# One attention and mixture-of-experts layer: POOL normalises the contexts from a copy that ScalarE makes, and VectorE takes only the reciprocal

## The reference

```
result = embeddings @ w_qkv                      # q, k, v
scores = einsum('bnqd,bnkd->bnqk', q, k) / sqrt(h)
probs  = softmax(scores, axis=-1)
ctx    = einsum('bnqk,bnkd->bnqd', probs, v)
x = layernorm(x + ctx)
scores = sigmoid(gates); top 8 of scores + expert_bias; selected / sum * 2.826
y = sum over experts of (silu(x Wg) * (x Wu)) Wd * combine, plus the shared network
x = layernorm(x + y)
```

## Time and profile before

| | |
|---|---|
| median of 3 runs | 723.49 us (723.25 to 724.71) |
| profiled execution, its own time | 725.11 us |
| its span | 723.4 us |
| attention, until the last pair is transposed | to about 393 us |
| feed-forward part | from about 393 us |
| busy, share of the span | TensorE 95%, VectorE 71%, ScalarE 57%, POOL 44% |

### The profile page before, as it was taken

How to read it: one execution, slowest core, us unless ns; L and a number is a source line. 1 busy time by engine, 2 the same in 40 slices (tenths; PEclk the granted TensorE clock), 3 DMA queues, 4 the chain that set the end, 5 groups by cost and what they waited for, 6 DMA issues and landing times. The chain is left out here.

```text
span 723.4 us, 13286 instructions
## 1 busy us (share of the span) xinstructions
PE 687.6 (95%) x3494; PEld 361.9 (50%) x3494; DVE 515.3 (71%) x1085; ACT 415.6 (57%) x779; POOL 321.2 (44%) x371
## 2 busy tenths in 40 slices
PE   2899999999999999999997999999999999999995
PEld 1343333433434334343323767666676767676662
DVE  1889988999999999999953546557565655656343
ACT  2068877988879888787886424334343434334321
POOL 3033342423424252252230756665565646666563
PEclk8569999999999999999999999999999999999998
DMA  6832251422414233241105023050606032140600
GB/s 184 257 98 89 84 156 34 140 70 82 155 53 148 68 100 110 82 137 52 46 5 202 33 108 128 22 227 0 248 0 245 3 145 103 50 198 9 239 1 29
DMA packets 34279, 74.89 MB, mean 104 GB/s; under 512 B 4144, under 2 KB 13488, under 8 KB 30032
## 3 DMA queue, kind: packets, MB, share of 16 engines
q1 hardware_dynamic: 33440, 72.38, 29.1%
q0 software_dynamic: 816, 2.23, 1.1%
HBM read 58.61 MB, written 15.99 MB: 103 GB/s over the span
## 5 line engine op out<-in xcount | busy, mean ns | idle before, releaser
L743 ACT ACTIVATE probs<-ps_k 128x512 f32<-128x512 f32 x500 | 262.6, 605 | 51.7 <-PE ps_k L849 47.5
L786 DVE TENSOR_REDUCE maxima<-ps_bank 128x1 f32<-128x512 f32 x384 | 245.4, 682 | 27.5 <-PE ps_bank L842 22.4
L1085 POOL TENSOR_TENSOR hidden<-gated,weights 128x512 f32<-128x512 f32 x128 | 167.0, 1311 | 124.2 <-DVE gated L1167 108.4
L1115 ACT ACTIVATE silu<-ps_gate 128x512 f32<-128x512 f32 x136 | 81.3, 598 | 176.9 <-PE ps_gate L1209 176.6
L1167 DVE TENSOR_TENSOR gated<-silu,ps_up 128x512 f32<-128x512 f32 x128 | 87.0, 685 | 105.2 <-PE ps_up L1209 69.7
L842 PE MATMUL ps_bank<-k_aug,q_aug 32*128 32x512 f32 x384 | 147.9, 513 | 12.5 <-DMA q_aug<-q_rows 8.8
L849 PE MATMUL ps_k<-q_aug,k_aug 32*128 32x512 f32 x500 | 154.2, 489 | 4.0 <-ACT probs L743 2.2
L862 PE MATMUL ps_ctx<-probs,v_ones 128*32 128x512 f32 x1024 | 138.8, 614 | 0.9 <-ACT probs L743 0.9
L1234 PE MATMUL ps_y<-hidden,nets_down 128*128 128x512 f32 x272 | 137.1, 591 | 0.0
L849 PEld LDWEIGHTS ps_k<-q_aug,k_aug 32*128 32x128 f32 x500 | 64.0, 185 | 124.3 <-ACT probs L743 107.2
L1206 PE MATMUL ps_gate<-x1T_high,nets_low 128*128 128x512 f32 x136 | 96.5, 710 | 0.0
(11 more groups left out here) (117 smaller groups left out, 648.9 us busy)
## 6 DMA issues: line engine op xcount, KB each, us to landing
weights<-combine_rows SPq DMA_DIRECT2D x32, 1024.0 KB, 7.5
k_aug<-k_rows SPq DMA_DIRECT2D x32, 256.0 KB, 2.7
q_aug<-q_rows SPq DMA_DIRECT2D x32, 256.0 KB, 2.9
q_rows<-qk_high SPq DMA_DIRECT2D x16, 256.0 KB, 2.9
k_rows<-qk_high SPq DMA_DIRECT2D x16, 256.0 KB, 3.6
net_raw<-w_nets POOLq DMA_DIRECT2D x17, 128.0 KB, 2.4
xT_sb<-xT SPq DMA_DIRECT2D x8, 256.0 KB, 2.9
q_rows<-qk_low SPq DMA_DIRECT2D x8, 256.0 KB, 3.1
```

The lines of the kernel that those rows point to most:

```text
L743: act.activation(probs[:, t, h, :], score_slot(i, last)[:], ACT.Exp, scale=ATT_SCALE).then_inc(exp_done, 1)
L786: dve.tensor_reduce(maxima[:, parity, TILES * h + t:TILES * h + t + 1], bank("q", (i - UNIT * AHEAD) % SCORES)[:], AX_X, ALU.max).then_inc ...
L1085: pool.tensor_tensor(hidden[:, s % RING, :], gated[:, s % UP_RING, :], r.weights[:, e, :], ALU.mult).then_inc(hidden_done, 1)
L1115: act.activation(silu[:, s % UP_RING, :], ps_gate[s % 2][:], ACT.Silu).then_inc(silu_done, 1)
```

## The change

ScalarE copies the nine needed columns of each head from the transposed bank to SBUF (context_raw) right behind the exponential of position 38 or 53, and that copy gives the bank back. VectorE takes one reciprocal of the 32 sums out of that copy, behind maximum 40 or 55 (written as CONTEXT_AFTER + 2) instead of behind 38 or 53. POOL multiplies in two instructions and then adds as before.

```
-def normalise_context(dve, c, pair, wait_added, src):
-
-    turned = src[:].rearrange("p (t h c) -> p t h c", t=TILES, h=GROUP)
-    dve.wait_ge(c.turned, pair + 1)
-    for j, at in enumerate(V_COLUMN):
-        dve.reciprocal(c.inverse[:, j], turned[:, :, :, at + HEAD])
-    dve.drain()
+def stage_context(act, c, pair, src, wait_ready):
+
+    act.wait_ge(c.turned, pair + 1)
+    if wait_ready:
+        act.wait_ge(c.ready, PAIR * pair)
+    turned = src[:].rearrange("p (n j c) -> p n j c", n=TILES * GROUP, j=PAIR)
+    act.copy(c.context_raw[:], turned[:, :, :, 0:HEAD + 1]).then_inc(c.staged, 1)
+
+
+def invert_context(dve, c, pair, wait_ready):
+    dve.wait_ge(c.staged, pair + 1)
+    if wait_ready:
+        dve.wait_ge(c.ready, PAIR * pair)
+    dve.reciprocal(c.inverse[:], c.context_raw[:, :, :, HEAD]).then_inc(c.inverted, 1)
+
+
+def add_context(pool, c, stream, pair, b, second, wait_added=True):
+
+    pool.wait_ge(c.inverted, pair + 1)
     if wait_added:
-        dve.wait_ge(c.added, pair)
-    for j, at in enumerate(V_COLUMN):
-        last = dve.tensor_tensor(c.context[:, :, j], turned[:, :, :, at:at + HEAD],
-                                 c.inverse[:, j].unsqueeze(3).to_broadcast([P, TILES, GROUP, HEAD]),
-                                 ALU.mult)
-    last.then_inc(c.ready, 1)
-
-
-def add_context(pool, c, stream, pair, b, second):
-
-    pool.wait_ge(c.ready, pair + 1)
+        pool.wait_ge(c.added, pair)
+    for j in range(PAIR):
+        pool.tensor_tensor(c.context[:, :, j],
+                           c.context_raw[:, :, j, 0:HEAD].rearrange("p (t h) e -> p t h e", t=TILES),
+                           c.inverse[:, :, j].rearrange("p (t h) -> p t h", t=TILES).unsqueeze(3)
+                           .to_broadcast([P, TILES, GROUP, HEAD]),
+                           ALU.mult).then_inc(c.ready, 1)
+    pool.wait_ge(c.ready, PAIR * (pair + 1))
...
+                            if i == CONTEXT_AFTER[0] and not first:
+                                stage_context(act, c, 2 * b - 1, bank("context", 0), True)
+                            if i == CONTEXT_AFTER[1]:
+                                stage_context(act, c, 2 * b, bank("context", 1), not first)
...
-                        if at == CONTEXT_AFTER[0] and not first:
-                            normalise_context(dve, c, 2 * b - 1, True, bank("context", 0))
-                        if at == CONTEXT_AFTER[1]:
-                            normalise_context(dve, c, 2 * b, not first, bank("context", 1))
+                        if at == CONTEXT_AFTER[0] + 2 and not first:
+                            invert_context(dve, c, 2 * b - 1, True)
+                        if at == CONTEXT_AFTER[1] + 2:
+                            invert_context(dve, c, 2 * b, not first)
...
-                    pe.wait_ge(c.ready, 2 * b + n)
+                    pe.wait_ge(c.staged, 2 * b + n)
...
+            stage_context(act, c, 2 * BATCHES - 1, c.ps_turned, True)
...
-            normalise_context(dve, c, 2 * BATCHES - 1, True, c.ps_turned)
+            invert_context(dve, c, 2 * BATCHES - 1, True)
```

More of the change, by code:

```diff
@@ L240, in __init__ @@
         self.context_T = ctx.enter_context(nc.sbuf_tensor("context_T", [P, PAIR, SEQ], F32))
-        self.inverse = ctx.enter_context(nc.sbuf_tensor("inverse", [P, PAIR, TILES, GROUP], F32))
+        self.inverse = ctx.enter_context(nc.sbuf_tensor("inverse", [P, TILES * GROUP, PAIR], F32))
         self.context = ctx.enter_context(nc.sbuf_tensor("context", [P, TILES, PAIR, GROUP, HEAD], F32))
+        self.context_raw = ctx.enter_context(nc.sbuf_tensor("context_raw", [P, TILES * GROUP, PAIR, HEAD + 1], F32))
         self.ps_turned = ctx.enter_context(nc.psum_tensor("ps_turned", [P, SEQ], F32))
@@ L245, in __init__ @@
         self.turned = ctx.enter_context(nc.semaphore("context_turned"))
+        self.staged = ctx.enter_context(nc.semaphore("context_staged"))
+        self.inverted = ctx.enter_context(nc.semaphore("context_inverted"))
         self.ready = ctx.enter_context(nc.semaphore("context_ready"))
@@ L663, in body @@
                     if g == 3:
-                        add_context(pool, c, stream, 2 * b, b, 0)
+                        add_context(pool, c, stream, 2 * b, b, 0, not first)
                     if first and g > 0:
```

## The result

Over 20 runs of each kernel the median is 724.26 us with the change (718.55 to 733.96) and 726.07 us without it (722.54 to 733.36). The ratio is 0.9945, with an interval of 0.9919 to 0.9972; it leaves out as slow the five runs of the changed kernel that took over 1.5% more than its fastest, and none of the kernel before, while the medians over all 20 runs of each give 0.9975. The same code, run again with the first group of experiments (re_after), gave 725.65 against 726.83, ratio 0.9998 [0.9961, 1.0034]. So the change is worth something between nothing and 0.8%. The forecast was 715.0 us, with a range of 711.5 to 719.0; the measured time lies above the range.

The account below looks back on a forecast made before the run. It took TensorE's waits for VectorE in the attention part, then ScalarE's, as the bound. Gains of 3.96, 3.22 and 1.29 made 8.5 us, from a median of 723.49 to 715.0 us; range 711.5 to 719.

Parts of the forecast that it names:

- Place 1: Behind position 38: TensorE waits only for VectorE; value matmuls come 0.66 us earlier in batches 1 to 6, 3.96 us.
- Place 2: Behind position 53: TensorE waits for ScalarE, then VectorE; 0.76 us of waiting less 0.30 of copy gains 0.46.
- 7 x 0.46: The gain behind position 53 summed over batches 0 to 6: 3.22 us.
- TensorE meets the next wait sooner: Rival: the gain behind position 53 is swallowed further on, leaving about 4.0 us, 719.5; chance 0.05.
- a dear copy: Same rival's other cause: a copy of 0.6 us or more cancels the gain behind position 53; shared chance 0.05.
- The last batch: Earlier bank release lets the transposes of x1 start 0.44 us and those of combine 0.85 us earlier, 1.29 together.
- third rival: A shorter stall in the last batch removes 3.41 us at half clock: 10.2 us gained, 713.3; chance 0.14.
- New stretches of half clock: A listed sign of being wrong: new stretches of TensorE at half clock would appear; no size or chance given.
- POOL: Per pair two 128x128 multiplications, 0.73 to about 1.8 us, hidden in 6.98 us of idle time; costed at nothing.
- the sixteenth pair: At the feed-forward start, copy and table load precede the first silu; hidden with 0.3 us to spare.
- faster: The whole kernel gains over 0.2% (1.4 us); chance 0.91, against same 0.03 and slower 0.06.

Follow-up runs that it names:

- place1_only: The new scheme behind position 38 and for the sixteenth pair, the kernel before's scheme behind position 53; 722.36 us against 726.83 before.
- narrow_exp: The changed kernel with exponentials 57 to 59 over only 256 of 512 columns in batches 1 to 7; 723.70 us against 726.02 before.
- place2_only: The new scheme behind position 53 alone, the kernel before's scheme behind position 38; 730.98 us against 726.83 before.
- weigh_early: The changed kernel with the value matmuls from behind position 56 put behind position 55, ahead of k56; 715.17 us against 726.02 before.
- weigh_copy: The changed kernel with value matmuls behind position 55 instead of 56 and position 53's copy behind exponential 54; 716.90 us against 726.27 before.
- weigh_recip: The changed kernel with value matmuls behind position 55 instead of 56 and position 38's reciprocal behind maximum 44; 713.94 us against 726.27 before.
- before_weigh: The kernel before with the value matmuls from behind position 56 put behind position 55; 722.44 us against 726.27 before.
- copy_late: The changed kernel with the copy of position 53 moved behind exponential 54; 719.19 us against 726.83 before.
- no_norm: The kernel before without normalisation and addition of the contexts, transposes kept, so a bound only; 712.77 us against 726.02 before.
- copy_only: The kernel before plus an unused ScalarE copy of 288 columns ahead of exponentials 39 and 54; 731.85 us against 726.02 before.
- recip_late: The changed kernel with position 38's reciprocal behind maximum 44 instead of 40; 724.39 us against 726.27 before.

## Why the prediction was wrong

The forecast was 9.3 us below the median that was measured. By the runs this comes apart as follows.

**The base, 2.6 us.** I subtracted from 723.49, the median of three runs. Over 20 runs the same kernel has 726.07. This part is no fault of the working, but a base of three runs of a kernel whose runs spread over 10 us was used as if it were firm.

**Place 1: right.** "q44 starts at 245.30, and the value matmuls come 0.66 us earlier": 0.70 in the trace. The reciprocal cost 0.26 as taken, the copy delays the next exponential by 0.28 where 0.30 was taken, and it hid behind VectorE. place1_only shows it by itself: its batches are 0.6 to 0.7 shorter, and at equal clock it is 4.4 us below the kernel before (3.96 and part of the last batch were forecast). The copy's estimate of 0.54 us from the Trainium skill, "ScalarE: Activation LUTs", Rules for kernel authors, was too high: its row has 0.40 to 0.47, and from start to start it costs 0.28.

**Place 2: the term "7 x 0.46" was mis-sized.** The step is "so the trio takes its 0.66 and the value matmuls start at 256.63 instead of 257.09: 0.46 gained". That holds as far as it reaches; against place1_only the changed kernel has them 0.47 earlier (15.26 and 15.73 behind k score 36). I stopped reading there. Three positions on, k62 meets exponential 59, and of the 0.47 there are 0.12 left (17.26 and 17.38). The slot had been free in time only because q59 was late. A wait of TensorE that goes makes its next k scores earlier, while the exponentials start from k57 and don't follow. narrow_exp, where exponential 59 is quick, gives the 0.35 back, and place2_only shows the same loss without the new place 1. Seven times 0.35 is 2.5 us. The rival "TensorE meets the next wait sooner" named this. It shared a chance of 0.05 with a dear copy, given without following the slots to position 62, though the trace had the rows for that.

**The last batch: 0.7 instead of 1.29.** The bank of x1 gave 0.38 for 0.44. The transposes of combine gave 0.30 for 0.85, because combine itself came later: 1.36 behind the end of the matmuls ahead of the transposes (385.40 against 384.04) instead of 0.90 (384.32 against 383.42). I had held its time fixed.

**The clock: the step that failed.** Of place 2 I wrote "The copy goes onto the path in full: k56 at 254.47", and priced it by its time on the path alone, 0.30. What it did to TensorE's clock I put at nothing, without a reason; in the third rival the clock could only give. "New stretches of half clock" stood among the signs of being wrong, with no chance and no price, and this is the sign that came. k56's wait went from 0.24 to 0.56 us, and stretches of half clock appeared from positions 56 and 57. The runs vary this wait in both directions, and the half clock follows:

| wait of k56 for ScalarE | kernels | half clock, median us | at 0.50 in stretches that begin behind k56, profiled execution, us |
|---|---|---|---|
| none | weigh_early, weigh_copy, weigh_recip, before_weigh | 44.2, 46.5, 41.3, 46.2 | 0, 0, 0, 0 |
| about 0.25 | before, place1_only, copy_late, no_norm | 52.2 to 53.6, 53.3, 50.9, 42.7 | 0, 0, 3.4, 0 |
| about 0.55 | the change, re_after, place2_only, copy_only, narrow_exp, recip_late | 61.4, 64.6, 64.1, 68.5, 62.1, 57.8 | 10.2, 10.2, 13.7, 34.1, 6.8, 23.9 |

The last column has the stretches that begin within 1.7 us of the start of k56 in batches 0 to 6. The step from 0.25 to 0.55 is clear in both schemes of normalising, and all six profiled executions with the long wait have such stretches. The step from none to 0.25 is smaller, and no_norm does not follow it: with all of VectorE's context work gone it keeps the wait of 0.24 and has no more half clock than the kernels without it. So other waits count with it there; which ones was not tested. copy_only is the cleanest of them: the wait alone, with no gain anywhere, raises the half clock by 15 us and the time by 5.8. weigh_early is its counterpart: the change is kept, the wait is filled with matmuls, and the clock comes back. The changed kernel has 8 to 12 us more at half clock than the kernel before; at the slope of 0.38 that is 3 to 4.5 us.

The sum: 9.3 forecast too low, of which 2.6 is the base, 2.5 exponential 59, 0.6 the last batch, and some 3.6 remain, which the clock's 3 to 4.5 can fill. That k56's wait brings the half clock is shown; its size in us is an estimate from the slope. At equal clock the change is worth 4 to 6 us (719.6 and 721.5 against 725.2 to 725.8), and place 1 is nearly all of it.

The Trainium skill, "TensorE: Matmul & The Clock Gate", A second HAM failure mode: psum-queue depth-cycling, says of another kernel, in bf16, that small idle times between groups of matmuls are frequent enough for the clock to swing between its two levels. The runs here agree that short idle times can do this: 0.3 us more of waiting at one position in each batch raised the half clock from 53.6 to 68.5 us (copy_only).

**POOL, the sixteenth pair and the sign.** POOL was hidden, as forecast. At the start of the feed-forward part the first silu waits 0.43 us for TensorE, so the copy of the sixteenth pair is hidden as well. The profiled execution has a stretch of half clock there, from 393.72 on, with the table load at 395.01 in it; whether the later copy brings it no run tells. The forecast of "faster" holds by the interval of 0.9919 to 0.9972 alone, and not by that of re_after.

**The third rival** hoped that a shorter stall in the last batch would take away the stretch of half clock behind it. The stall for x1 is 0.78 us instead of 1.16, and the stretch is gone in the profiled execution of the changed kernel. But it is there in re_after, the same code with the same stall (370.52 to 373.93 at 0.50), so the shorter stall does not prevent it.

**What stays open.** Which part of the activity around position 56 the clock answers to was not tested further, nor why no_norm has so little half clock with k56's old wait. The half-clock time of one and the same kernel varies from 49 to 89 us among the 20 executions of the changed kernel, so single profiled executions tell where stretches fall, and the medians how much half clock there is. Why an undisturbed batch of place2_only is 0.17 longer than one of before (43.41 and 43.24) was not found; up to position 63 it is level with it.

## What to carry to other kernels

When a wait of one engine goes, follow the producer three or four more slots of every ring that it uses: the time gained is worth only what is left behind the next wait. And price a wait that is added on TensorE twice, as time on the path and as a thin place that the clock may answer. Here the second was the larger by the estimates (3 to 4.5 us, against 7 x 0.3 = 2.1 on the path). One number in an order table, which put ready matmuls in front of the wait, was worth 9 us (715.17 against 724.26). Where clock and structure mix, compare the length of undisturbed batches and the time at half clock apart, and take the base from as many runs as the result.

## What the hardware showed unexpectedly

- A wait of 0.55 instead of 0.24 us, once in a batch of 43 us in which TensorE's rows cover 42.2 to 42.7, moved the time at half clock from 53.6 to 68.5 us (copy_only). copy_only also has the copy ahead of exponential 39; place2_only, which has none there, shows 64.1 us.
- In place2_only the half clock came behind k56 in four batches running, 44.4 us apart. The longest stretches behind k56 were 23.89 us, in copy_only and in recip_late.
- One us at half clock cost 0.38 us of time between executions of one kernel (the change, 20 runs). The stretches of place2_only cost 1.0 to 1.1 us for 3.41.
- A reciprocal of 32 columns has a row of 0.34 us and takes 0.26 of VectorE, and a copy of 288 columns from PSUM has a row of 0.40 to 0.47 and takes 0.28 of ScalarE.
